# Segment attention's head in quarters, with statistics, queries and a last MLP in other places

## The reference

```
# layer 0: 16 heads of 8
xn  = layernorm(x, ln1);  q, k, v = split(xn @ sa_wqkv)
res = x + merge(softmax(mask(q k^T * C**-0.5)) v) @ sa_wproj + b
kv  = layernorm(ctx, ln2) @ ed_wkv;  q2 = layernorm(res, ln2) @ ed_wq
res = res + merge(softmax(q2 k2^T * C**-0.5) v2) @ ed_wproj + b
x   = res + relu(layernorm(tgt, ln3) @ ff_w1 + b1) @ ff_w2 + b2
# layer 1: 16 heads of 64, with memory tokens from ctx
mem = rms_norm(mean(ctx, 1)) @ to_mem_tokens_w      # broadcast to 16 tokens
k_m, v_m = keys and values of mem
q, k, v = split(rms_norm(x) @ to_qkv_w);  q, k = rope(q), rope(k)
kf, vf  = [k_m, persist, k], [v_m, persist, v]
x = x + softmax(mask(q kf^T * 64**-0.5)) vf @ to_out_w
a, g = split(rms_norm(x) @ ff_w1 + b1);  x = x + (silu(g) * a) @ ff_w2 + b2
```

## Time and profile before

| | us |
|---|---|
| three runs | 1264.57, 1267.42, 1268.15 |
| median | 1267.42 |
| profiled execution, its own time | 1259.12 |
| its span in the trace | 1256.5 |

### The profile page before, as it was taken

One profiled execution on the slowest core, in us unless ns is written; L12 is line 12 of the kernel. 1 busy time (PEld: TensorE's weight loads), 2 busy tenths in 40 slices (PEclk: granted clock), 3 DMA queues, 4 the chain that ended last, 5 costly groups with the idle time before them and its releaser, 6 DMA issues. The chain is left out here.

```text
span 1256.5 us, 38139 instructions
## 1 busy us (share of the span) xinstructions
PE 1122.8 (89%) x15980; PEld 757.1 (60%) x15980; DVE 910.4 (72%) x1730; ACT 752.5 (60%) x1077; POOL 837.2 (67%) x1235
## 2 busy tenths in 40 slices
PE   2888878999999999999999999999657699898985
PEld 1555645666666666666666666666442457575663
DVE  6788757887787887778877788777356768686813
ACT  1333476777777777777777777777612336363641
POOL 2687467887888878878788787871009887767400
PEclk9999888999999999999999999999979899999987
DMA  7200043232222323223223232121000000000000
GB/s 172 85 2 1 17 127 109 72 108 87 94 96 83 107 77 105 98 70 118 79 95 109 66 113 89 64 76 39 2 17 1 2 2 2 8 2 1 9 9 8
DMA packets 70790, 75.99 MB, mean 60 GB/s; under 512 B 21596, under 2 KB 65372, under 8 KB 70492
## 3 DMA queue, kind: packets, MB, share of 16 engines
q1 hardware_dynamic: 70620, 73.57, 18.8%
HBM read 32.89 MB, written 0.92 MB: 27 GB/s over the span
## 5 line engine op out<-in xcount | busy, mean ns | idle before, releaser
L1129 DVE TENSOR_REDUCE tops_sb<-ps_b 112x2 f32<-112x1000 f32 x378 | 453.3, 1199 | 151.9 <-PE ps_b L899 149.5
L1054 ACT ACTIVATE probs_sb<-ps_a 128x896 f32<-128x896 f32 x352 | 322.6, 916 | 118.5 <-PE ps_a L851 118.5
L842 PE MATMUL ps_d<-probs_sb,values_sb 128*32 128x112 f32 x6144 | 228.2, 266 | 0.6 <-ACT probs_sb L1054 0.5
L899 PE MATMUL ps_b<-keys_sb,queries_sb 64*112 64x500 f16 x756 | 160.8, 416 | 14.4 <-DVE tops_sb L1129 9.4
L226 POOL TENSOR_SCALAR context_sb<-context_sb,ln_sb 125x128 f32<-125x128 f32 x384 | 168.4, 456 | 7.7 <-POOL ln_sb L244 7.6
L842 PEld LDWEIGHTS ps_d<-probs_sb,values_sb 128*32 128x32 f32 x6144 | 135.0, 109 | 40.2 <-issue 7.2
L851 PEld LDWEIGHTS ps_a<-queries_sb,keys_sb 64*128 64x128 f16 x3072 | 125.1, 102 | 49.9 <-ACT probs_sb L1054 8.7
L851 PE MATMUL ps_a<-queries_sb,keys_sb 64*128 64x112 f16 x3072 | 141.0, 210 | 5.8 <-ACT probs_sb L1054 5.5
L867 PE MATMUL ps_c<-xs_t_sb,w_kv_sb 128*128 128x200 f32 (+1 forms) x384 | 123.6, 419 | 0.9 <-ACT xs_t_sb L1079 0.9
L938 PE MATMUL ps_c<-w_kv_sb,xs_t_sb 128*128 128x128 f32 x768 | 119.2, 292 | 1.1 <-ACT k_rows_sb L997 1.0
L761 POOL TENSOR_TENSOR k_split_sb<-k_rows_sb,k_split_sb 128x500 f16<-128x500 f32 x96 | 109.0, 1136 | 8.0
(11 more groups left out here) (267 smaller groups left out, 1902.6 us busy)
## 6 DMA issues: line engine op xcount, KB each, us to landing
keys_sb<-k_split_sb SPq DMA_DIRECT2D x288, 125.0 KB, 2.5
context_sb<-in_ctx SPq DMA_DIRECT2D x32, 750.0 KB
queries_sb<-q_split_sb SPq DMA_DIRECT2D x21, 112.0 KB, 5.8
keys_sb<-in_ones SPq DMA_DIRECT2D x3, 375.0 KB, 3.3
w_qk_sb<-in_w_qkv SPq DMA_DIRECT2D x1, 1024.0 KB, 11.5
queries_sb<-shift_sb SPq DMA_DIRECT2D x64, 1.8 KB
x_all_sb<-in_x SPq DMA_DIRECT2D x2, 448.0 KB
out<-y_sb SPq DMA_DIRECT2D x8, 112.0 KB
```

The costliest lines, as they stand in the source:

```text
L842: last = nc.tensor.matmul(o_bank[32 * (g % 4):32 * (g % 4) + 32, 112 * (g // 4):112 * (g // 4) + 112], values[r][:, k, g, :], probs[k % 2] ...
L899: last = nc.tensor.matmul(scan_of(b + d, n)[0:2 * T, 512 * e:512 * e + 500], queries_of(b + d, e, g), keys[(r + d) % 3][64 * e:64 * e + 64 ...
L1054: nc.scalar.activation(probs[s % 2][:].rearrange("p (e n) -> p e n", e=2), halves(ps_a[:, :]), ACT.Exp).then_inc(Q["probs_ready"], 1)
L1129: nc.vector.tensor_reduce(tops[(b + d) % 2][:, :, n // 3, n % 3], scan_of(b + d, n)[0:2 * T, :].rearrange("p (e n) -> p e n", e=2)[:, :, 0 ...
```

## The change

It has four parts, and computes the same.

1. Stage 1, DVE: the statistics of every iteration (`context_counted`, `rows_counted`, `rsqrt`) stand ahead of the four sums instead of behind the scaling of the output.
2. Stage 2: at b = -2 PE's `queries_made(0)` stands at step 3 instead of ahead of step 0, and ACT's `queries_high(0)` at step 5 instead of 2; at b = -1 the scan of a step stands ahead of `rows_turn` and `queries_made` of that step on PE.
3. Stage 3's head: only the first quarter (four pairs and the memory row) is added, counted, scaled, transposed and written before the first slice. The rest is done by the functions `memory(n)` and `others(n)` on DVE behind the rotation of slice n: n = 0, 1, 4 memory tokens; n = 0 to 2 the adds of quarters 1 to 3; 3 to 5 their counting; 6 the aggregates and the scale (12 `BN_AGGR` and 12 further operations); 7 to 9 the scaling of quarters 1 to 3. On PE the memory products stand at n = 0, 1, 3, the values of iteration 0 at n = 6 to 13, the transposes of quarters 1 to 3 at n = 11 to 13. The scaled rows go to the tiles `s1` instead of `q1`, so POOL's clearing of `q1` no longer waits for the head.
4. In the last iteration the MLP of the iteration before has all its steps two slices earlier (`EARLIER` = 2) on PE, ACT and DVE.

```diff
@@ stage 1, DVE
+                        if i < 2:
+                            context_counted(i)
+                        else:
+                            rows_counted(2 * U * (i - 2), U * i)
...
                         for u in range(U):
                             wait("e0_ready", u + 1)
...
-                        if i < 2:
-                            context_counted(i)
-                        else:
-                            rows_counted(2 * U * (i - 2), U * i)
...
@@ stage 2, PE
                         if b == -2:
                             rows_turn(0)
-                            queries_made(0)
                         for s in range(KT):
+                            if b == -2 and s == 3:
+                                queries_made(0)
+                            d = 2 if s in AHEAD else 1
+                            if has(d):
+                                scan(UNITS[s], d)
                             if b == -1 and s % 3 == 0 and s < 9:
                                 rows_turn(s // 3 + 1)
                             if b == -1 and s % 3 == 1 and s < 9:
                                 queries_made(s // 3 + 1)
-                            d = 2 if s in AHEAD else 1
-                            if has(d):
-                                scan(UNITS[s], d)
@@ stage 2, ACT
-                            if b == -2 and s == 2:
+                            if b == -2 and s == 5:
                                 queries_high(0)
-                            if b == -2 and s == 5:
                                 queries_low(0)
@@ stage 3
+            ROW_AT, Y_AT, EARLIER = 6, 15, 2
+            FIRST_VALUES = {n: (n - 6) for n in range(6, 14)}
+            FIRST_TURNS = {11: 1, 12: 2, 13: 3}
@@ POOL
-                    pool.wait_ge(head_pe, 8)
                     nc.gpsimd.memset(q1[:] ...
@@ PE
+                    rows_turn(0)
                     for n in range(16):
                         projected(0, n)
-                        if n % 2 == 1:
-                            values1(0, n // 4, n // 2 % 2)
+                        memory(n)
+                        if n in FIRST_VALUES:
...
+                            values1(0, FIRST_VALUES[n] // 2, FIRST_VALUES[n] % 2)
+                        if n in FIRST_TURNS:
+                            rows_turn(FIRST_TURNS[n])
...
-                                mlp(i - 1, n)
+                                mlp(i - 1, n + EARLIER * (i == NIT - 1))
@@ DVE
+                    def others(n):
+                        if n in (0, 1, 2):
+                            rows_added(n + 1)
+                        if n in (3, 4, 5):
+                            rows_counted(n - 2)
+                        if n == 6:
+                            scales(U + 1, NPAIR + 1)
+                        if n in (7, 8, 9):
+                            rows_normed(n - 6)
+                    rows_added(0)
+                    rows_counted(0)
+                    scales(0, U + 1)
+                    rows_normed(0)
...
-                    memory_keys(0)
                     for n in range(16):
+                        if n == 15:
+                            memory_keys(0)
                         rotate(0, n)
+                        memory(n)
+                        others(n)
```

More of the change, by code:

```diff
@@ L1345, in _, with rows_turn @@
                         last.then_inc(head_pe, 1)
[L1346 to L1351 removed]
+                    def rows_turn(q):
@@ L1358, in _ @@
[L1358 to L1363 removed]
+                            last = nc.tensor.transpose(turn_bank(q)[:, 128 * u:128 * u + 128], normed_all[q][:, u, :], ident)
@@ L1646, in _, with rows_counted @@
-                    ve.wait_ge(mem_pe, 4)
-                    nc.vector.tensor_copy(mem_k[:], ps_b[:, 512:768].rearrange("p (j b) -> p j b", j=NJ)).then_inc(mem_dve, 1)
-                    ve.wait_ge(mem_dve, 5)
+                        nc.vector.tensor_tensor(rows, banks[4 + q].rearrange("p (u c) -> p u c", u=U), rows, ALU.add).then_inc(head_x, 1)
+                    def rows_counted(q):
+                        ve.wait_ge(head_x, q + 1)
+                        for pair in range(U * q, U * q + U):
+                            ins = nc.vector.bn_stats(st_all[:, stat_of(pair), :], x_all[:, pair, :])
+                        link(ins)
@@ new lines, in scales @@
+                    def scales(first, end):
+                        for n in range(first, end):
+                            ins = nc.vector.bn_aggr(mv_all[:, n, :], st_all[:, n, :])
+                        link(ins)
+                        ms, rstd, tmp = ms_all[:, 0, first:end], ms_all[:, 1, first:end], ms_all[:, 2, first:end]
+                        link(nc.vector.tensor_tensor(ms, mv_all[:, first:end, 0], mv_all[:, first:end, 0], ALU.mult))
+                        link(nc.vector.tensor_tensor(ms, ms, mv_all[:, first:end, 1], ALU.add))
+                        rsqrt(ve, link, rstd, ms, tmp, EPS1)
```

138 lines of the change are left out of this document (75 added, 63 removed).

## The result

The changed kernel took 1246.92 us at the median (1245.77 to 1250.92), the kernel before 1265.99 beside it (1256.77 to 1268.15): a ratio of 0.9875, 95% interval 0.9836 to 0.9914, or -15.8 us (-10.9 to -20.8). The forecast was -6.4 us and 1261.0, the range 1253 to 1270; the kernel is faster than the range allows.

A forecast was written before the change was run, and what follows sets the result against it. PE fills the middle of the span; the edits lie before and behind it, where no engine is full. The parts' +3.4 - 1.6 - 3.4 - 4.8 = -6.4 us took the median from 1267.4 to 1261.0, range 1253 to 1270.

The forecast's parts named there:

- the step had 5.9: Stage 1, iteration 1: statistics wait for POOL; scores 4.7 us later with iteration 0's gain included, 5.9 against iteration 1 before.
- the term of 1.25: Stage 1, iterations 0 and 2: statistics hide in the wait ahead of the fourth sum, spread keys start 1.25 us earlier.
- a rival: Whole kernel: the gains are given back, with the earlier queries shifting nothing (+0.35); total -0.2 us, 1267.2; chance 0.23.
- 14.4 at the first rotation: Head of stage 3: less work ahead of the first slice, so POOL starts 14.4 us earlier, 13.2 at low PE clock.
- 5.6 for slice 6: Stage 3, slice 6: aggregates and small operations take 5.7 us with the rotation, +3.3 after what POOL has buffered.
- 3.52 for slices 7 to 9: Stage 3, slices 7 to 9: scalings beside rotations make POOL's pace 3.52 us, 1.36 over its 2.157, 4.1 for three.
- The rival with the clock: Stage 3 slices: PE's clock falls, projections slow down, +10.8 us; total +4.4, 1271.8; chance 0.11.
- The Trainium skill's rule: Stage 3 slices: shared ports block for one operation only; four scalings cost POOL 0.80 us, part 3 gives -5.1.
- 4.65 of the 4.8: The end: up and down projections 2.25 us earlier, plus 2.55 if the down projection keeps full clock; -4.8 together.
- The base: Whole kernel: the sum is made against the profiled 1259.12 us, 8.3 below the median 1267.42; the same difference is added.

The follow-up runs named there:

- warm: The changed kernel with two extra matmuls on PE ahead of the MLP's transposition in iterations 1 and 2 of stage 3; 0.9885 of the kernel before.
- early_pool: The changed kernel with POOL's ten small operations on the statistics moved to the end of iteration 0 of stage 1; median 1239.68 us, 0.9817 of the kernel before.
- mixed: The changed kernel with iteration 1's statistics in stage 1 directly ahead of the scaled output; median 1249.44 us, 0.9872 of the kernel before.

## Why the prediction was wrong

The direction and three of the four mechanisms held; the sizes did not. The column of traces is the difference of the means over the stretch that a part touches, between the traces with it and without it; those that have another edit in the stretch are left out.

| part | forecast | alone, timed | in traces |
|---|---|---|---|
| 1, statistics | +3.4 | -0.9 | -1.5 (145.0 against 146.5 at the last scaled output) |
| 2, queries | -1.6 | -5.4 | -2.6 in the scans of stage 2, -1.9 at the start of stage 3 |
| 3, head | -3.4 | -2.1 | -1.4 to the next iteration, -1.8 behind it |
| 4, end | -4.8 | -8.6 | -5.6 |

**Part 1 is the step that failed**, and with it the sum. Its iteration 1 was right in kind: the wait, who is queued behind it, the slowed add, PE's low clock. It cost 4.6 in the first traces (4.1 on the means), where the step had 5.9, from the dear half of its own range. Wrong was the term of 1.25 for iterations 0 and 2. I took the start of the spread keys as the gain, bounded by when the keys are there. But DVE's two spread keys also became shorter (2.14 instead of 2.8), since they now begin with POOL's and not in the middle of its run, and with 0.62 instead of 2.56 us of idle PE kept its clock. In the traces iteration 2 shrank from 29.85 (mean of seven) to 26.77, by 3.1, and iteration 0 by 2.2. So the step's +5.9 - 1.25 - 1.25 was +4.1 - 2.2 - 3.1, and another -0.4 came in iteration 3, where nothing was counted: a gain instead of a loss. That the idle time removed takes a stretch at half clock with it was counted for the down projection in part 4, and not here: PE's idle 2.57 was only read as a wait. How the gain of these iterations divides between the keys and the clock, no run tells.

**Part 2** was right in kind (the round fell from 6.8 to 5.8 us) and too small, because the one trace of before showed the short form of the round. It was 6.8 in three, 8.0 in two and 9.1 in two of seven traces in the old order, and 5.8 in ten of thirteen in the new. Of the 2.6 gained some 0.75 is lost again at the end of stage 2: from the last scan to the start of stage 3 the old order takes 25.9 to 26.4 us, the new one 25.9 to 27.8. So the gain didn't quite survive until 918 us, which the prediction had left to a rival.

**Part 3** was right by row: 14.1 of 14.4 at the first rotation, 5.6 for slice 6, 3.52 for slices 7 to 9. The rival with the clock happened in part (the projections of slices 3 to 5 at 0.50, +1.5) without becoming the bound. The Trainium skill's rule that the prediction had weighed against the rows ("SBUF — State Buffer", section "Who interferes with whom") would have given 0.80 more for four scalings; POOL's pace of 3.52, 1.36 more, came again. That the iteration behind the head gets shorter (98.1 against 100.0 on the mean) is in the traces, and not explained.

**Part 4** was right: 4.65 of the 4.8 from add 1 to add 2, and 0.95 more behind it, where among others the output's 64 matmuls take 7.31 (L1471) instead of 7.66.

**The base** was the other error. I added 8.3 us to carry a profiled time to the median, but took every difference from the one profiled execution, a lucky one. Where it showed the short form of a clock stall, as in the query round, a part that removes the stall was worth more than that trace could say.

Open is the remainder. The places above sum to some -12 us (with -1.9 for part 2) and the timed ratios to -15.8 and -18.5, with intervals that reach -10.9 and -14.3; parts 2 and 4 also gained more when timed alone than in the traces. What starts the long form of a stall in one execution and not in the next isn't settled; `warm` did not tell.

## What to carry to other kernels

A step that is moved ahead of others takes its semaphore waits with it: move what it waits for first, as `early_pool` does, and the same move is worth some 9 us instead of under 2 (1.5 and the 7.7 of the wait). An idle stretch of PE cost its length and often the slow matmuls behind it here, so count both wherever one is shortened. And before a difference of 1% is forecast from a trace, it helps to know where in the scatter that trace lies.

## What the runs showed of the hardware

Executions of the same program differ by up to 1%, and with them the granted clock of PE. In the traces the difference lies in places where the clock stays at 0.50 for longer behind the same idle time: the stretch from add 0 to add 1, with every instruction the same, took 68.5 us at a granted clock of 0.98 or 71.6 at 0.93, and nothing between, in eighteen traces. In 29 timed runs of the kernel before on one chip, the nine under 1261 us had 0.958 to 0.965 over the whole span, the six above 1267 us 0.954 to 0.960.

One DVE operation with both inputs in SBUF (128x512, f32) took 6.79 us while POOL ran six operations of its own in a row, in `mixed`. A pair of them took 2.14 when the first began just ahead of POOL's run, and 2.8 when it began in the middle of it. An add of the same size takes 0.69 alone.
